# Who adds up the weight blocks: VectorE, or transfers that accumulate and are issued by GpSimd

## The reference

```
x = x + tanh(g_xattn) * wkv(time_decay, time_first, k = layernorm(x), v = ctx)
x = x + tanh(g_ffn)   * ffn(layernorm(x))

ffn(x): up_gate = x @ W1.T; up_lin = x @ W3.T        # W1, W3: 2048 x 512
        hidden  = fwht(silu(up_gate) * up_lin)       # Walsh-Hadamard transform of 2048
        out     = hidden @ W2.T                      # W2: 512 x 2048
```

## Time and profile before

| | |
|---|---|
| median of 3 runs | 1072.43 us (1069.78 to 1075.06) |
| the profiled execution | 1073.34 us, span 1071.6 us |
| mean granted TensorE clock | 0.983 |
| TensorE busy | 1001.8 us, 93% |
| VectorE busy | 826.3 us, 77% |
| ScalarE busy | 430.6 us, 40% |
| GpSimd busy | 221.1 us, 21% |
| moved by DMA | 201.74 MB, mean 188 GB/s |
| instructions | 18143 |

### The profile page before, as it was taken

One profiled execution on the slowest core, in us unless ns is written; L12 is line 12 of the kernel. 1 busy time (PEld: TensorE's weight loads), 2 busy tenths in 40 slices (PEclk: granted clock), 3 DMA queues, 4 the chain that ended last, 5 costly groups with the idle time before them and its releaser, 6 DMA issues.

```text
span 1071.6 us, 18143 instructions
## 1 busy us (share of the span) xinstructions
PE 1001.8 (93%) x6826; PEld 684.3 (64%) x6892; DVE 826.3 (77%) x1364; ACT 430.6 (40%) x720; POOL 221.1 (21%) x164
## 2 busy tenths in 40 slices
PE   5698997988789999999999899999999999999998
PEld 2364443456557776777767576776767677777775
DVE  7847899999999996789758796789759995653334
ACT  6755341335134452454234452454234443432221
POOL 0130000002321233212421033212421133211111
PEclk9989998999899999999999999999999999999999
DMA  9966517645755556255654456355654434434341
GB/s 357 334 258 255 197 40 275 239 174 176 290 222 178 198 185 231 97 178 197 238 195 143 156 195 233 88 174 197 230 204 139 165 150 158 158 142 154 142 154 40
DMA packets 40908, 201.74 MB, mean 188 GB/s; under 512 B 8944, under 2 KB 18288, under 8 KB 29808
## 3 DMA queue, kind: packets, MB, share of 16 engines
q1 hardware_dynamic: 40816, 200.52, 51.8%
HBM read 171.12 MB, written 29.38 MB: 187 GB/s over the span
## 4 chain that ended last, share of the span: by engine, by line
PE 63%; DVE 22%; issue 7%; ACT 3%; DMA 3%; SPq 1%; another core or an unknown queue 0%; DVEq 0%; ACTq 0%
PE pl L730 7%; PE pl L728 7%; PE pl L729 7%; PE po L740 7%; PE po L742 7%; PE pg L728 6%; PE pg L730 6%; PE pg L729 6%; PE po L751 4%; PE po L749 2%; DVE work L1487 2%; DVE eb L1245 1%; DVE x L1394 1%; DVE work L1575 1%; DMA bv<-x_tok 1%
## 5 line engine op out<-in xcount | busy, mean ns | idle before, releaser
L1677 POOL TENSOR_TENSOR work<-work 128x512 bf16<-128x512 f32 x112 | 163.9, 1463 | 744.5 <-DVE work L1575 738.2
L740 PE MATMUL po<-work,w 128*128 128x512 f16 x456 | 173.0, 379 | 1.8 <-DVE x L1394 0.7
L742 PE MATMUL po<-work,w 128*128 128x512 f16 x456 | 172.8, 379 | 0.0
L1042 ACT ACTIVATE work<-work 128x256 f32<-128x256 f32 x168 | 68.6, 416 | 231.6 <-DVE work L1487 231.4
L728 PE MATMUL pg<-wts 128*128 128x256 f16 x448 | 122.5, 273 | 22.6 <-DVE work L1487 21.7
L1487 DVE TENSOR_TENSOR work<-pl,wts 128x256 f32<-128x256 f32 x168 | 65.3, 416 | 80.2 <-PE pl L730 78.8
L729 PE MATMUL pl<-wts 128*128 128x256 bf16 x448 | 122.7, 274 | 0.0
L728 PE MATMUL pl<-wts 128*128 128x256 f16 x448 | 122.7, 274 | 0.0
L730 PE MATMUL pl<-wts 128*128 128x256 f16 x448 | 122.7, 274 | 0.0
L728 PE MATMUL pl<-xn,wts 128*128 128x256 f16 x448 | 122.7, 274 | 0.0
L730 PE MATMUL pl<-xn,wts 128*128 128x256 f16 x448 | 122.6, 274 | 0.0
(11 more groups left out here) (200 smaller groups left out, 2133.4 us busy)
## 6 DMA issues: line engine op xcount, KB each, us to landing
wts<-up_stage SPq DMA_DIRECT2D x56, 2048.0 KB, 7.9
up_stage<-wts SPq DMA_DIRECT2D x8, 1024.0 KB, 8.0
up_stage<-wts SPq DMA_DIRECT2D x16, 512.0 KB, 3.2
ev<-ctx_t SPq DMA_DIRECT2D x7, 1024.0 KB, 10.1
xin<-x_t SPq DMA_DIRECT2D x7, 1024.0 KB, 7.2
bv<-x_tok SPq DMA_DIRECT2D x7, 1024.0 KB, 9.3
out_t<-x SPq DMA_DIRECT2D x7, 1024.0 KB, 4.4
wts<-w_t SPq DMA_DIRECT2D x11, 512.0 KB, 4.9
```

The lines of the kernel that those rows point to most:

```text
L740: pe.matmul(po[:, d, :], w2h[:, j, d * P:d * P + P], hh[:, b, :], start=start, stop=False, skip_group_check=True)
L742: pe.matmul(po[:, d, :], w2l[:, j, d * P:d * P + P], hh[:, b, :], start=False, stop=False, skip_group_check=True)
L1042: act.activation(sg[:, slot, cols], src, ACT.Silu).then_inc(acted, 1)
L1677: pool.tensor_tensor(hl[:, b, :], hf[:, slot, :], hh[:, b, :], ALU.subtract).then_inc(pair_lo, 1)
```

## The change

VectorE no longer makes the weights' sums. GpSimd issues for each unit three transfers that add to what lies at their destination (`add_up`): the first adds half of the unit, read again from HBM, to the other half in SBUF (512 elements a partition), the second and the third add 256 elements a partition from SBUF to SBUF. Each waits for the one before. The signs of the block sums on x's side are turned over so that all sums of the weights are additions; in slot 1 the products then come out negative, and ScalarE's silu and VectorE's product take that back. So that the halves lie together, the weights' layout in `wts` is slots before channel blocks. `weight_parts` stays with VectorE and waits for all three transfers. `SUMS_AT`, `LATE_SUMS` and `BETWEEN` are set anew, `EARLY_ADDS` (units 0 to 10, after GpSimd's last work on W2) and `LATE_ADDS` (11 to 15, after the subtractions of pairs 0 to 4 of chunk 1) place the transfers in GpSimd's list. The token normalising (`tok_norm`) moves from tile 2 to 3, the second channel sum of chunk 1 from tile 12 to 11, there behind the parts, and SP puts unit 7 and loads unit 10 ahead of the load of pair 1.

```diff
-FIRST_AT = dict(tok=2, tok_norm=2, ...
+FIRST_AT = dict(tok=2, tok_norm=3, ...
-                sum_var=12, var=(13, 0), rsqrt=13, norm=14, next_tok=12)
+                sum_var=11, var=(13, 0), rsqrt=13, norm=14, next_tok=12)
-SUMS_AT = {3: (0,), 5: (1,), 9: (2,), 10: (3,), 11: (4,), 12: (5,), 13: (6,)}
-LATE_SUMS = {0: (7,), 1: (8,), 2: (9,), 3: (10, 11), 4: (12, 13), 5: (14, 15)}
-BETWEEN = {0: (), 1: (), 2: (9,), 3: (11,), 4: (13,), 5: (15,)}
+SUMS_AT = {4: (0,), 5: (1,), 6: (2,), 8: (3,), 9: (4,), 11: (5,), 12: (6,), 13: (7,)}
+LATE_SUMS = {0: (8,), 1: (9,), 2: (10,), 3: (11,), 4: (12, 13), 5: (14, 15)}
+BETWEEN = {0: (), 1: (), 2: (10,), 3: (11,), 4: (13,), 5: (15,)}
+EARLY_ADDS = range(0, 11)
+LATE_ADDS = {0: (11,), 1: (12,), 2: (13,), 3: (14,), 4: (15,)}
...
-        wts = sb("wts", [P, WP, 4, KT, PW], F16)
+        wts = sb("wts", [P, WP, 4, PW // P, KT, P], F16)
...
-            put_sums(6)
-            load_again(9)
+            for n in range(6, 8):
+                put_sums(n)
+                load_again(n + TRAWS)
             load_pair(Run(2), 1)
...
-                act.activation(sg[:, slot, cols], src, ACT.Silu).then_inc(acted, 1)
+                act.activation(sg[:, slot, cols], src, ACT.Silu, scale=(1.0, -1.0)[slot]).then_inc(acted, 1)
...
-                dve.tensor_tensor(s1, a21, a22, ALU.add).then_inc(xsum, 1)
+                dve.tensor_tensor(s1, a22, a21, ALU.subtract).then_inc(xsum, 1)
-                dve.tensor_tensor(s2, s1, a11, ALU.subtract).then_inc(xsum, 1)
+                dve.scalar_tensor_tensor(out=s2, in0=s1, scalar=-1.0, in1=a11, op0=ALU.mult,
+                                         op1=ALU.subtract).then_inc(xsum, 1)
-                dve.tensor_tensor(s4, a12, s2, ALU.subtract).then_inc(xsum, 1)
+                dve.scalar_tensor_tensor(out=s4, in0=a12, scalar=-1.0, in1=s2, op0=ALU.mult,
+                                         op1=ALU.subtract).then_inc(xsum, 1)
...
-            def weight_sums(n):
-                b = unit_blocks(n)
-                dve.wait_ge(traw_loaded[n % TRAWS], 16 * (n // TRAWS + 1))
-                dve.tensor_tensor(b[:, 0:2, :].rearrange("p k (s n) -> p s k n", s=2), ...
-                dve.tensor_tensor(b[:, 2:4, P:], b[:, 2:4, P:], b[:, 0:2, 0:P], ALU.subtract).then_inc(wsum, 1)
-                dve.tensor_tensor(b[:, 2:4, 0:P], b[:, 2:4, 0:P], b[:, 2:4, P:], ALU.subtract).then_inc(wsum, 1)
             def weight_parts(n):
+                dve.wait_ge(summed[n % TRAWS], 48 * (n // TRAWS + 1))
...
-                    dve.tensor_tensor(hf[:, 1, :], sg[:, 1, :], hf[:, 1, :], ALU.mult).then_inc(pair_hidden, 1)
+                    dve.scalar_tensor_tensor(out=hf[:, 1, :], in0=sg[:, 1, :], scalar=-1.0, in1=hf[:, 1, :],
+                                             op0=ALU.mult, op1=ALU.mult).then_inc(pair_hidden, 1)
...
+            def add_up(n):
+                w, p = units[n]
+                b, counted = unit_blocks(n), 48 * (n // TRAWS)
+                half = unit // 4
+                pool.wait_ge(traw_loaded[n % TRAWS], 16 * (n // TRAWS + 1))
+                pool.dma_start(b[:, :, 0:half], raw_in[w][p][:, 2 * half:].rearrange("p (r n) -> p r n", r=2),
+                               accum_op=ALU.add).then_inc(summed[n % TRAWS], 16)
+                pool.wait_ge(summed[n % TRAWS], counted + 16)
+                pool.dma_start(b[:, 1, half:], b[:, 0, 0:half], accum_op=ALU.add).then_inc(summed[n % TRAWS], 16)
+                pool.wait_ge(summed[n % TRAWS], counted + 32)
+                pool.dma_start(b[:, 0, half:], b[:, 1, half:], accum_op=ALU.add).then_inc(summed[n % TRAWS], 16)
             def ffn():
                 for i in range(11, TILES):
                     tile_clamp(i)
+                for n in EARLY_ADDS:
+                    add_up(n)
...
+                    if run.is_front(2):
+                        for n in LATE_ADDS.get(p, ()):
+                            add_up(n)
```

More of the change, by code:

```diff
@@ L210, in flamingo_block @@
         rstd_log, rstd_first = sem("rstd_log"), sem("rstd_first")
-        wsum, wsum_hi, wsum_lo = sem("wsum"), sem("wsum_hi"), sem("wsum_lo")
+        summed = [sem(f"summed{i}") for i in range(TRAWS)]
+        wsum_hi, wsum_lo = sem("wsum_hi"), sem("wsum_lo")
         ring_loaded = [sem("ring_loaded0"), sem("ring_loaded1")]
@@ L302, in hi_of @@
             w, p = units[n]
-            return wts[:, p, kind_of[w], :, :].rearrange("p a b -> p (a b)")
+            return wts[:, p, kind_of[w], :, :, :].rearrange("p s k n -> p (s k n)")
         def lo_of(n):
             w, p = units[n]
-            return wts_lo[:, p, kind_of[w] + 1, :, :].rearrange("p a b -> p (a b)")
+            return wts_lo[:, p, kind_of[w] + 1, :, :, :].rearrange("p s k n -> p (s k n)")
         def weights(p, i, w, k):
             sums, k0, slot = WEIGHTS_OF[i]
-            place, cols = RING + 2 * (p % 2) + sums, slice(slot * P, slot * P + P)
-            return wts[:, place, 2 * w, k0 + k, cols], wts_lo[:, place, 2 * w + 1, k0 + k, cols]
+            place = RING + 2 * (p % 2) + sums
+            return wts[:, place, 2 * w, slot, k0 + k, :], wts_lo[:, place, 2 * w + 1, slot, k0 + k, :]
         def operand(run, i, k):
@@ L449, in load_pair @@
                 place = RING + 2 * (p % 2)
-                sp.dma_start(wts[:, place:place + 2, :, :, :].rearrange("p s a k n -> p s (a k n)"),
+                sp.dma_start(wts[:, place:place + 2, :, :, :, :].rearrange("p u a s k n -> p u (a s k n)"),
                              stage[p % PAIRS]).then_inc(ring_loaded[p % 2], 16)
@@ L647, in up @@
                 wait(pe, freed, run.tile(j - uses))
-                p, col, cols = j // (PW // P), j % (PW // P) * P, run.cols(j)
+                p, slot, cols = j // (PW // P), j % (PW // P), run.cols(j)
                 for k in range(KT):
-                    hi, lo = wts[:, p, 2 * w, k, col:col + P], wts_lo[:, p, 2 * w + 1, k, col:col + P]
+                    hi, lo = wts[:, p, 2 * w, slot, k, :], wts_lo[:, p, 2 * w + 1, slot, k, :]
                     nh, nl = xnh[run.par][:, k, cols], xnl[run.par][:, k, cols]
@@ L1457, in ffn @@
                     hidden_lo(run, j)
-                    if at(j, "sum_var"):
-                        channel_sum(ahead, 1)
                     if at(j, "resid"):
@@ L1470, in ffn @@
                     for n in SUMS_AT.get(j, ()):
-                        weight_sums(n)
                         weight_parts(n)
+                    if at(j, "sum_var"):
+                        channel_sum(ahead, 1)
                     if at(j, "next_tok"):
@@ L1627, in _ @@
         def _(pool):
+            raw_in = {"w1": w1_in, "w3": w3_in}
             def channel_sum(run, which):
```

17 lines of the change are left out of this document (5 added, 12 removed).

## The result

The change makes the kernel slower: 1109.98 us median (1108.04 to 1111.47) against 1072.22 of before, ratio 1.0346 with a 95% interval of 1.0318 to 1.0374. The forecast was 1059 us, with a range of 1045 to 1083. The profiled execution has a span of 1109.1 us and a mean granted clock of 0.968 (before 1071.6 and 0.983).

What follows compares the result with a forecast made beforehand. VectorE was taken to bound about 115 to 345 us, TensorE all that follows. Gains of 28.0 less 3.3 (start), 7.0 (pair 4) and 3.3 (pair 5) left 14.4: 1073.3 - 14.4 = 1058.9, said as 1059; range 1045 to 1083.

Steps and rivals of the forecast that it cites:

- VectorE is the bound, sums out: From about 115 to 345 us VectorE bounds the kernel; dropping the weights' sums takes 27.4 us of work from it.
- ceiling: Gain up to chunk 1's pair 7 if every sum is there when VectorE asks: 28.0 us.
- X = 9.3: Time in us of one unit's three serial adds on GpSimd, priced as 4.9 + 2.2 + 2.2.
- the bound from above, 14.7: Upper bound in us for one unit's three adds: three loads of 512 KB at 4.9.
- Free up to X = 11: Early adds end at 200 or near 212 us, before GpSimd's first subtraction for chunk 1 at 218: no loss.
- Pair 4: Chunk 1: channel sum behind unit 14's adds comes X - 2.3 = 7.0 us late, and TensorE stands.
- Pair 5: Chunk 1: unit 15's sums and a channel sum come X - 6 = 3.3 us late, both together.
- Pairs 1 to 3 have room: Chunk 1: some 11 us are left between adds, so nothing is late while X is under 11.
- Rival C: Adds bound the stretch from X = 12.4, slower than before; at X = 14 the run takes 1093 us; chance 0.17.
- The start, priced at 3.3: Group 2 of chunk 0: VectorE waits 1.3 us for unit 1 and 2 for unit 6, loss 3.3.
- B: As rival: X of 12, 1071 us, no difference; chance 0.10. "Their B" is the first join of chunk 2's pair 0.
- D: Rival: VectorE wasn't the bound, so removing its sums moves nothing, 1073 us; chance 0.04.

Runs made afterwards that it cites:

- e1: The change without its 48 accumulating transfers, the weights' sums left out; VectorE's parts wait for the load alone: 1038.27 us, ratio 0.9682.
- e8: The kernel before with only the token normalising moved from tile 2 to tile 3: 1065.79 us, ratio 0.9961.
- e15: The change with units 0 and 15 summed by VectorE, one add for units 1 to 10 and 14, three for 11 to 13: 1050.76 us, ratio 0.9798.
- e11: The change with the per-token factors sent to DRAM as contiguous 32 bytes per partition in place of single 4-byte elements: 1101.83 us, ratio 1.0282.
- e3: The change with the same 48 transfers as plain copies, nothing added, so the sums are wrong: 1080.32 us, ratio 1.0074.
- e4: The change with SP's eight ring loads for chunk 1 cut from 2 MB to 256 KB each: 1091.42 us, ratio 1.0178.
- e12: The change with the edits of e3 and e4 together, plain copies and 256 KB ring loads: 1076.64 us, ratio 1.0038.
- e5: The change with GpSimd issuing only each unit's first add, without waiting; VectorE makes the other two sums: 1060.19 us, ratio 0.9887.
- e2: The change's layout, signs and order, but VectorE makes all three sums and GpSimd issues no transfers: 1061.12 us, ratio 0.989.
- e16: e14 with the two loads for chunk 3 ahead of unit 14's first add cut from 1 MB to 256 KB each: 1076.74 us, ratio 1.0057.
- e14: The change with accumulating transfers only for units 11 to 15; VectorE sums units 0 to 10: 1080.96 us, ratio 1.0081.
- e10: The change with GpSimd making each unit's three sums itself by tensor_tensor instructions, no accumulating transfers: 1068.63 us, ratio 0.9973.

## Why the prediction was wrong

First joins of the change against those of e1, step by step; the sum is the 74.5 us between their B. "Forecast" is the loss that the prediction gave the step.

| step | forecast | measured |
|---|---|---|
| up to pair 0's first join (group 2, early adds) | 3.3 | 36.5 |
| pair 0 to pair 1 (subtractions behind the early adds) | 0 | 10.3 |
| pairs 1 to 4 | 0 | 1.1 |
| pair 4 to 5 | 7.0 | 20.7 |
| pair 5 to 6 and 7 | 3.3 | 6.0 |

- **VectorE is the bound, sums out: right.** 27.0 us less busy time; ceiling 34.2 and not 28.0. The working undercounted the normalising of the tokens (3.4; e8 shows 4.2 to 8.5) and chunk 1 (14.5; in e1 pair 0 to pair 7 is 106.0 against 123.5, so 17.5).
- **X = 9.3: the step that failed.** For a unit alone it was fair (period 8.6, to the last landing 10.8). The error was to use one X for all units. The earlier trace rows are medians over the run; the adds run beside SP's bulk, and there a mean unit of the early queue took 15.2 (14.0 without the waits for loads) and unit 14 18.9 from its first issue to the start of the channel sum. Even the bound from above, 14.7, was too low, for it too was made of medians. The DMA share of 0.56 was in view and not put into the price.
- **"Free up to X = 11": wrong with it.** The early adds ended at 263 and not near 212. VectorE waited for them five times (29.0 and 6.8 us), the first time 7.2 us for unit 0, for which the forecast had no wait, and pair 1's first join waited 9.66 for GpSimd's subtraction.
- **Pair 4: right in place and form.** It was to be late by X - 2.3; with 18.9 that is 16.6, and 17.63 was measured.
- **Pair 5: right in form.** TensorE waited 4.57 at the matmul of the variance, where about 3 was forecast, and VectorE 6.52 for unit 15.
- **Pairs 1 to 3 have room: right.** 1.1 us, with units of about 9 to 11; e15 lets three adds stand there, and no loss shows.
- **Rival C was what came**, with a chance of 0.17: at X = 14 it had 1093, at 11 us for each further microsecond about 1106 at the measured 15.2, and 1110 was measured. Its direction and mechanism are right; that the total comes so near is in part luck, since its terms miss both ways. It had 28 us at X = 14 for the start and pair 0 (measured 46.8), 2.5 for each of pairs 1 to 3 (1.1 in all), and 20 for pairs 4 and 5 (26.7); and VectorE waited for units 0, 1, 5, 6 and 8, not 1, 2, 6 and 7.
- **The start, priced at 3.3.** A further cause was not foreseen at all: the factors' transfer of single elements, 8.2 us (e11).
- **A slip in the chances.** "Same" was given 0.13, though B and D alone make 0.14; nothing hangs on it.

Of the 71.7 us that the adds cost, 29.7 go with accumulation as against copying (e3) and 18.6 with the ring loads beside it (e4); these overlap, since with copies the ring loads cost 3.7 (e12). Some 38 remain with copies and thin loads (e12), at the units that have SP's other transfers beside them. e5 shows it from the other side: with one add a unit and no wait on GpSimd it is level with e2. It drops two thirds of the transfers together with the waiting, so the serial chain isn't separated from the number of transfers.

TensorE's clock fell with the waits: where it stood waiting more, in 100 to 215 us, the granted clock is 0.88 against 0.99 in e1. For the same 6826 matmul records it is busy 1005.7 us in the change and 993.1 in e1. How much of the 71.7 us that makes isn't shown, since much of it can lie under the waits.

## What to carry to other kernels

Price a transfer that others wait for by the load beside it, not by its median alone: ask what the other queues issue in the microseconds before it, and give each place of the schedule its own X. A chain of small dependent transfers in an in-order queue multiplies that delay; take its first link only, or leave to the idle engine those units for which nobody waits yet (e15), and keep such a chain out of the queue ahead of work that TensorE needs. When cost meets slack in a sum, work the sum also at the price where slack ends: here the rival at X = 14 had the sign and the mechanism. And run the new order without the new mechanism, as e2 does: it alone was faster than before, and without it e15's whole gain would have been put down to the adds.

## What the runs showed of the hardware

- Accumulating transfers issued by GpSimd took 5.1 us (256 KB) and 3.0 us (128 KB) from issue to next issue with little beside them, plain copies 3.3 and 2.3; the third add landed 2.7 us after its issue. The 48 of them went in 8960 packets against 2816.
- Issued within 3 us behind 2 to 4 MB of SP's transfers the same 256 KB took 10 to 12 us (11.4 for unit 10 in the change, 10.1 in e16, 12.2 and 11.8 for unit 14 in the change and e14), a plain copy 8.1 (unit 14 in e3). Beside 1024 elements of 4 bytes it took 14.6, and 5.1 when these went as 128 pieces of 32 bytes (e11).
- Two-input instructions of GpSimd on f32 in SBUF went with VectorE's two-input instructions at 1666 in place of 1225 ns in the mean (128x1024, L1413 in e10), and with 17.1 in place of 13.1 us for the 16 one-input instructions at L1423; over the kernel VectorE was busy 24.9 us longer with 48 more instructions of GpSimd.
